# First keys and queries moved in another order, with edits to the softmax sums, the router and the experts' first load

## The reference, cut to what matters

```
# cross-attention, 16 heads of 32, 8192 keys for each batch
q, k, v = heads(layernorm(x) @ Wq), heads(ctx @ Wk), heads(ctx @ Wv)
x = x + (softmax(q k^T / sqrt(32)) v) @ Wo
# causal self-attention: softplus amplitude (normalised per head) and tanh phase
x = x + amp_phase_attention(layernorm(x))
# experts: 16 of them, the best 2 for each token, 64 places for each expert and batch
g = softmax(layernorm(x) @ w_router)           # 16 scores for each token
p1, p2, e1, e2 = top_k(g, 2)                   # place = running count of the expert
x = x + sum over both of p * expert(e, row)    # silu(row @ gate) * (row @ fc) @ proj
```

## Time and profile before

| | us |
|---|---|
| median of 3 runs | 2043.98 |
| the profiled execution, its own time | 2044.43 |
| its span in the profile | 2042.7 |
| PE busy | 1894.5 (93%) |
| DVE busy | 1726.3 (85%) |
| ACT busy | 1469.4 (72%) |
| mean granted clock of PE | 0.971 of full |

### The profile page before, as it was taken

The page is one execution under the profiler, slowest core; times in us unless marked ns, Lnnn a source line. Parts: engine busy times, 40 slices in busy tenths (PEclk is TensorE's granted clock), DMA queues, the critical chain, the costliest instruction groups (busy, mean ns, idle before and its releaser), DMA issues.

```text
span 2042.7 us, 30924 instructions
## 1 busy us (share of the span) xinstructions
PE 1894.5 (93%) x11702; PEld 779.7 (38%) x11702; DVE 1726.3 (85%) x1509; ACT 1469.4 (72%) x1671; POOL 46.3 (2%) x57
## 2 busy tenths in 40 slices
PE   7799999999999999999999999999998989997593
PEld 3333333333333333333333333333332445555482
DVE  5589999999999999788999999999999587786354
ACT  2288888888888888668888888888886546452120
POOL 2000000000000000000000000000000000001103
PEclk9899999999999999999999999999999989999797
DMA  5533332233333323322323333323240000006574
GB/s 192 200 100 92 89 97 84 78 88 90 91 92 86 97 78 105 92 78 58 98 78 83 88 89 93 89 83 99 62 151 15 22 1 2 1 31 228 201 261 145
DMA packets 112584, 194.55 MB, mean 95 GB/s; under 512 B 10288, under 2 KB 63536, under 8 KB 112432
## 3 DMA queue, kind: packets, MB, share of 16 engines
q1 hardware_dynamic: 109872, 184.12, 30.6%
q0 software_dynamic: 2560, 8.39, 1.2%
HBM read 108.58 MB, written 50.33 MB: 78 GB/s over the span
## 4 chain that ended last, share of the span: by engine, by line
PE 80%; DVE 8%; DMA 4%; issue 3%; ACT 2%; SPq 1%; POOL 1%; POOLq 0%; ACTq 0%; DVEq 0%
PE ps L1055 21%; PE ps L1227 21%; PE ps L972 11%; PE ps L969 11%; PE ps L1286 3%; DVE dacc L1657 2%; PE ps L1088 2%; PE ps L1127 2%; PE ps L1083 1%; PE ps L1042 1%; PE ps L1296 1%; DMA kscr<-wsm 1%; PE ps L1152 1%; DMA kst<-kscr 1%; PE ps L1142 1%
## 5 line engine op out<-in xcount | busy, mean ns | idle before, releaser
L1489 ACT ACTIVATE pt<-ps,bias 128x1024 f32<-128x1024 f32 x1024 | 1110.0, 1114 | 222.8 <-PE ps L1227 222.2
L1657 DVE TENSOR_TENSOR dacc<-dacc,pt 128x2048 f32<-128x2048 f32 x504 | 1152.8, 2287 | 50.1 <-ACT pt L1489 25.5
L1227 PE MATMUL ps<-qst,kst 128*128 128x512 f16 x2048 | 614.0, 382 | 20.6 <-ACT pt L1489 19.7
L1055 PE MATMUL ps<-pt,vt 128*32 128x512 f32 x4096 | 494.5, 600 | 1.8 <-ACT pt L1489 1.8
L1227 PEld LDWEIGHTS ps<-qst,kst 128*128 128x128 f16 x2048 | 178.2, 98 | 427.8 <-ACT pt L1489 133.3
L969 PE MATMUL ps<-wsm 128*128 128x512 f16 x1152 | 313.7, 383 | 14.6 <-DVE wsm L1615 10.7
L972 PE MATMUL ps<-wsm 128*128 128x512 f16 x1152 | 312.1, 381 | 5.2 <-ACT vt L1341 2.8
L1055 PEld LDWEIGHTS ps<-pt,vt 128*32 128x32 f32 x4096 | 106.8, 109 | 267.0 <-issue 243.2
L969 PEld LDWEIGHTS ps<-wsm 128*128 128x128 f16 x1152 | 113.0, 99 | 155.8 <-DVE wsm L1615 10.7
L972 PEld LDWEIGHTS ps<-wsm 128*128 128x128 f16 x1152 | 112.9, 98 | 145.2 <-issue 5.3
L1600 DVE SCALAR_TENSOR_TENSOR wsm<-ps,wsm 128x512 f16<-128x512 f32 x128 | 87.7, 686 | 31.8 <-ACT wsm L1337 31.7
(11 more groups left out here) (192 smaller groups left out, 1188.2 us busy)
## 6 DMA issues: line engine op xcount, KB each, us to landing
kscr<-wsm SPq DMA_DIRECT2D x128, 256.0 KB, 3.5
kst<-kscr SPq DMA_DIRECT2D x128, 256.0 KB, 3.5
kst<-kst SPq DMA_DIRECT2D x128, 256.0 KB, 3.4
wsm<-in_ctx SPq DMA_DIRECT2D x32, 768.0 KB, 4.8
qst<-qscr SPq DMA_DIRECT2D x32, 128.0 KB, 2.9
xbuf<-xn SPq DMA_DIRECT2D x16, 256.0 KB, 6.4
wsm<-in_gate SPq DMA_DIRECT2D x8, 512.0 KB, 4.7
wsm<-in_fc SPq DMA_DIRECT2D x8, 512.0 KB, 5.9
```

The source lines that it names most:

```text
L1055: p = e.matmul(ps[32 * h:32 * h + 32, 4 + n % 2, :], vt[:, kb % 2, ch, c:c + 32], pt[:, (2 * i + h // 2) % 6, h % 2, :], start=ch == 0, st ...
L1227: p = e.matmul(ps[:, 2 * half + h2, :], kst[:, kb % 2, h, ch * 128:ch * 128 + 128], qst[:, h, :], start=True, stop=True)
L1489: e.activation(pt[:, (2 * i + half) % 6], ps[:, 2 * half:2 * half + 2, :], ACT.Exp, bias=bias[:, 4 * kb + ch:4 * kb + ch + 1], scale=SCORE ...
L1657: e.tensor_tensor(own_heads, own_heads, probs, ALU.add).then_inc(S["add"], 1)
```

## The change

- Start-up: `k_move` is split for block 0 into `k_store` and `k_load`. The load takes both halves of the partitions from DRAM, without the copy within the core. The order on SP's queue is now: store keys 0, keys 1; load keys 0, keys 1; store queries 0, keys 2; load queries 0, keys 2; store queries 1, keys 3; load queries 1, keys 3; store queries 2, queries 3; load queries 2, queries 3.
- Last key block of batch 1 (16 steps): in the third and fourth chunk of each group DVE no longer adds; PE sums these probabilities with `ones`, four matmuls in a step, straight into the bank of `finish`.
- Last query tile of self-attention (four groups n): DVE adds two of the four key tiles and masks the last one, and PE sums the other two key tiles itself, 8 more matmuls for each n.
- Router: rT now turns the tile x3 as it is, without waiting for statistics; mean and scale are applied to the 16 logits: logit is now two operations, and one product of `wr` with `ones` (colsum) and its negation (negsum) are new, once. In the order of the slots rT, rC, router and logit of tile 6 come later, and at the end rT and rC of tile 7 come ahead of stat and lroot.
- Top 2: 'first' has 3 operations, 'second' 6, 'shares' 4. 'first' needs no exponential, and for the second half of the tokens 'shares' comes after the rows are known. xn3 of the last tile is made behind 'cum'.
- Experts: the four loads of `xe` have 1, 3, 5 and 7 blocks in place of 4 each.

The core of the diff (left out: counts that follow from it, two new small buffers, a constant that is folded into an index):

```diff
@@ -30,6 +30,7 @@
+PARTS = ((0, 1), (1, 4), (4, 9), (9, 16))
@@ -379,6 +380,12 @@
+ON_PE = [i for i in range(STEPS - 16, STEPS) if i % 4 > 1]
+
+
+def added(i):
+
+    return i + 1 - sum(x <= i for x in ON_PE)
@@ -491,6 +498,9 @@
+if not kept:
+    late = {4: ["wo0"], 5: ["wo1"], 6: ["x3", "stat"], 7: ["lroot"], 8: ["lnr", "xn3"], 10: ["rT"], 11: ["rC"],
+            13: ["router"], 14: ["logit"]}
@@ -503,6 +513,11 @@
+if a == 1 and k == 4:
+    out.append(("colsum", 0, fill((1,))))
+    empty((1,), "lg", 1)
+if a == 1 and k == 5:
+    out.append(("negsum", 0))
@@ -510,7 +525,7 @@
-out.append((("rank", "odds", "shares", "first", "second")[(6, 8, 9, 11, 13).index(k)], 0))
+out.append((("rank", "odds", "first", "second", "shares")[(6, 8, 9, 11, 13).index(k)], 0))
@@ -592,13 +607,15 @@
-for step in ("x3", "stat", "lroot", "lnr", "xn3", "rT", "rC", "router", "logit"):
+for step in ("x3", "rT", "stat", "rC", "lroot", "lnr", "router", "logit"):
...
-for what in ("rank", "odds", "shares", "first", "second"):
+for what in ("rank", "odds", "first", "second"):
...
+follow(7, "xn3")
...
+out.append(("shares", 1))
@@ -805,6 +824,16 @@
+def k_store(g):
+    e.wait_ge(S["klo"], g + 1)
+    e.dma_start(kscr[0, g], khl[:, g % 2]).then_inc(S[f"kw{g}"], 16)
+
+def k_load(g):
+    e.wait_ge(S[f"kw{g}"], 16)
+    for half, name in ((0, "kr"), (64, "ku")):
+        e.dma_start(kst[half:half + 64, 0, 4 * g:4 * g + 4, :],
+                    kscr[0, g].rearrange("(h r) t k -> (r t) h k", h=4)).then_inc(S[f"{name}{g}"], 16)
+
@@ -828,17 +857,21 @@
-k_move(0, 0)
-k_move(0, 1)
+k_store(0)
+k_store(1)
+k_load(0)
+k_load(1)
...
+k_store(2)
...
-k_move(0, 2)
+k_load(2)
...
+k_store(3)
...
-k_move(0, 3)
+k_load(3)
...
+q_store(0, 3)
...
-q_store(0, 3)
@@ -884,9 +917,9 @@
-for q in range(4):
-    e.dma_start(xe[:, 4 * q:4 * q + 4, :],
-                xbuf[512 * q:512 * q + 512, :].rearrange("(x p) c -> p x c", p=128)).then_inc(S[f"qx{q}"], 16)
+for q, (lo, hi) in enumerate(PARTS):
+    e.dma_start(xe[:, lo:hi, :],
+                xbuf[128 * lo:128 * hi, :].rearrange("(x p) c -> p x c", p=128)).then_inc(S[f"qx{q}"], 16)
@@ -1027,10 +1060,10 @@
-at = bank(("finish", b, g))
-e.wait_ge(S["add"], 256 * b + 240 + 4 * g + 4)
+at = 6 + BANK_OF["finish", b, g] % 2 if b else bank(("finish", b, g))
+e.wait_ge(S["add"], added(256 * b + 240 + 4 * g + 3))
...
-    p = e.matmul(ps[32 * h:32 * h + 32, at, :], ones[:, 0:32], dacc[:, 4 * g + h, :], start=True,
+    p = e.matmul(ps[32 * h:32 * h + 32, at, :], ones[:, 0:32], dacc[:, 4 * g + h, :], start=b == 0,
@@ -1054,11 +1087,16 @@
+if i in ON_PE:
+    at = bank(("finish", 1, g)) if ch == 2 else 6 + BANK_OF["finish", 1, g] % 2
+    for h in range(4):
+        p = e.matmul(ps[32 * h:32 * h + 32, at, :], ones[:, 0:32], pt[:, (2 * i + h // 2) % 6, h % 2, :],
+                     start=ch == 2, stop=False)
...
-if what in ("turn", "p01", "p23", "p4", "qkT", "wo", "woT", "rT", "router", "score", "scoreT", "cum", "pT"):
+if what in ("turn", "p01", "p23", "p4", "qkT", "wo", "woT", "rT", "router", "colsum", "score", "scoreT", "cum", "pT"):
@@ -1141,9 +1179,14 @@
+alone = range(2, 4) if t == 7 else ()
...
-                 keysum[:, u, h4, :] if qb else pT[:, u, h4, 0:128], start=True, stop=True)
+                 keysum[:, u, h4, :] if qb else pT[:, u, h4, 0:128], start=True, stop=not alone)
+for k in alone:
+    for h4 in range(4):
+        p = e.matmul(ps[32 * h4:32 * h4 + 32, 6, g * 128:g * 128 + 128], ones[:, 0:32],
+                     pT[:, u, h4, k * 128:k * 128 + 128], start=False, stop=k == 3)
@@ -1191,10 +1234,15 @@
-    e.wait_ge(S["xn3"], t + 1)
+    e.wait_ge(S["x3"], t + 1)
...
-        p = e.transpose(ps[:, ev[2], k * 128:k * 128 + 128], xn3[:, t, k * 128:k * 128 + 128], ident[:])
+        p = e.transpose(ps[:, ev[2], k * 128:k * 128 + 128], xs[:, t, k * 128:k * 128 + 128], ident[:])
...
+elif what == "colsum":
+    e.wait_ge(S["late"], 48)
+    for k in range(4):
+        p = e.matmul(ps[:, 1, 0:16], ones[:], wr[:, k, :], start=k == 0, stop=k == 3)
+    p.then_inc(S["rM"], 1)
@@ -1485,7 +1533,7 @@
-e.wait_ge(S["add"], i - 2)
+e.wait_ge(S["add"], added(i - 3))
@@ -1670,6 +1718,8 @@
+if f:
+    e.wait_ge(S["att"], f)
@@ -1791,6 +1841,12 @@
+if n >= 28:
+    e.tensor_tensor(keysum[:, u], block[0], block[1], ALU.add).then_inc(S["dve"], 1)
+    e.wait_ge(S["dve"], own.up())
+    e.tensor_tensor(block[3], block[3], trib[:].unsqueeze(1).to_broadcast([128, 4, 128]),
+                    ALU.mult).then_inc(S["cut"], 1)
+    return
@@ -1827,44 +1883,60 @@
-    e.wait_ge(S["rM"], t + 1)
-    e.tensor_copy(lg[:, t, :], ps[:, ev[2], 0:16]).then_inc(S["lg"], 1)
+    e.wait_ge(S["lstat"], t + 1)
+    e.tensor_scalar(shift[:], negs[:], mv[:, t, 0:1], rs[:, t:t + 1], ALU.mult, ALU.mult).then_inc(S["dve"], 1)
+    e.wait_ge(S["dve"], own.up())
+    e.wait_ge(S["rM"], t + 2)
+    e.scalar_tensor_tensor(out=lg[:, t, :], in0=ps[:, ev[2], 0:16], scalar=rs[:, t:t + 1], in1=shift[:],
+                           op0=ALU.mult, op1=ALU.add).then_inc(S["lg"], 1)
+elif what == "negsum":
+    e.wait_ge(S["rM"], 1)
+    e.tensor_scalar(negs[:], ps[:, 1, 0:16], -1.0, None, ALU.mult).then_inc(S["lg"], 1)
...
-    e.wait_ge(S["lg"], 4 * t + 4)
+    e.wait_ge(S["lg"], 4 * t + 5)
...
+elif what in ("first", "second"):
+    tiles, k = slice(4 * t, 4 * t + 4), 0 if what == "first" else 1
+    back = iot[:, 1, :].unsqueeze(1).to_broadcast([128, 4, 16])
+    e.wait_ge(S["const"], 1)
+    if k == 0:
+        e.wait_ge(S["lgs"], t + 1)
+        e.scalar_tensor_tensor(out=w3[:, tiles], in0=lg[:, tiles], scalar=0.0, in1=back, op0=ALU.is_equal,
+                               op1=ALU.mult).then_inc(S["dve"], 1)
+    else:
+        e.wait_ge(S["pexp"], t + 1)
+        e.scalar_tensor_tensor(out=lg[:, tiles], in0=ohb[:, 0, tiles], scalar=-2.0, in1=pp[:, tiles],
+                               op0=ALU.mult, op1=ALU.add).then_inc(S["dve"], 1)
+        e.wait_ge(S["dve"], own.up())
+        e.tensor_reduce(tp[:, 1, tiles], lg[:, tiles], AX.X, ALU.max).then_inc(S["dve"], 1)
+        e.wait_ge(S["dve"], own.up())
+        e.tensor_tensor(w3[:, tiles], lg[:, tiles], wide(tp[:, 1, tiles]), ALU.is_equal).then_inc(S["dve"], 1)
+        e.wait_ge(S["dve"], own.up())
+        e.tensor_tensor(w3[:, tiles], w3[:, tiles], back, ALU.mult).then_inc(S["dve"], 1)
+    e.wait_ge(S["dve"], own.up())
+    e.tensor_reduce(ei[:, k, tiles], w3[:, tiles], AX.X, ALU.min).then_inc(S["dve"], 1)
+    e.wait_ge(S["dve"], own.up())
+    mark = e.tensor_tensor(ohb[:, k, tiles], wide(ei[:, k, tiles]), back, ALU.is_equal)
+    if k:
+        mark.then_inc(S["ohb"], 1)
+    else:
+        mark.then_inc(S["dve"], 1)
+        e.wait_ge(S["dve"], own.up())
...
+    e.tensor_reduce(tp[:, 0, tiles], pp[:, tiles], AX.X, ALU.max).then_inc(S["dve"], 1)
+    e.wait_ge(S["dve"], own.up())
...
-    e.tensor_tensor(pp[:, tiles], pp[:, tiles], wide(v8[:, tiles]), ALU.mult).then_inc(S["dve"], 1)
+    e.tensor_tensor(tp[:, :, tiles], tp[:, :, tiles], v8[:, tiles].unsqueeze(1).to_broadcast([128, 2, 4]),
+                    ALU.mult).then_inc(S["dve"], 1)
...
-elif what in ("first", "second"):
...
@@ -1917,7 +1989,8 @@
-adds(i)
+if i not in ON_PE:
+    adds(i)
```

More of the change, by code:

```diff
@@ L484, in follow @@
             out.append(("router", f, bank, fill((bank,))))
-            empty((bank,), "lg", f + 1)
+            empty((bank,), "lg", f + 2)
         elif step == "logit":
@@ L673, in build @@
         wr = sb("wr", [128, 4, 16], F32)
+        negs = sb("negs", [128, 16], F32)
+        shift = sb("shift", [128, 16], F32)
         s1 = ExitStack()
@@ L917, in pool @@
             e.iota(iot[:, 0, :], pattern=[[1, 16]], base=0, channel_multiplier=0, allow_small_or_imprecise_dtypes=True)
-            e.iota(iot[:, 1, :], pattern=[[1, 16]], base=100, channel_multiplier=0,
+            e.iota(iot[:, 1, :], pattern=[[1, 16]], base=-100, channel_multiplier=0,
                    allow_small_or_imprecise_dtypes=True)
@@ L1269, in e_turn @@
                 s = x % 2
-                e.wait_ge(S[f"qx{x // 4}"], 128 + 16)
+                e.wait_ge(S[f"qx{next(q for q, (lo, hi) in enumerate(PARTS) if x < hi)}"], 128 + 16)
                 if x > 1:
@@ L1473, in self_piece @@
                     if t:
-                        e.wait_ge(S["rM"], t)
+                        e.wait_ge(S["rM"], t + 1)
                     e.activation(aR[:], ps[:, ev[2], :], ACT.Copy).then_inc(S["rC"], 1)
@@ L1655, in adds @@
                 else:
-                    e.wait_ge(S["add"], i)
+                    e.wait_ge(S["add"], added(i - 1))
                     e.tensor_tensor(own_heads, own_heads, probs, ALU.add).then_inc(S["add"], 1)
@@ L1844, in self_piece @@
                     e.wait_ge(S["dve"], own.up())
-                    e.tensor_tensor(pp[:, tiles], pp[:, tiles], wide(v8[:, tiles]), ALU.mult).then_inc(S["dve"], 1)
+                    e.tensor_tensor(tp[:, :, tiles], tp[:, :, tiles], v8[:, tiles].unsqueeze(1).to_broadcast([128, 2, 4]),
```

(28 more changed lines are left out.)

## The result

| | before | changed |
|---|---|---|
| median, us | 2044.01 (4 runs, 2043.13 to 2045.52) | 2026.64 (4 runs, 2023.89 to 2028.71) |
| ratio to before, 95% interval | | 0.9912 (0.9897 to 0.9927) |
| the profiled execution, own time / span | 2044.43 / 2042.7 | 2023.89 / 2022.1 |
| mean granted clock of PE | 0.971 | 0.978 |

The changed kernel is 17.4 us faster by the medians; 16.4 was forecast (2028.0, range 2023.5 to 2032.5). By the interval of the ratio the gain is 14.9 to 21.1 us. The profiled execution is the fastest of the four, so its differences have to be read against other executions before they are put down to the change.

The account below looks back on a forecast made before the run. PE was taken to bound the kernel in the main loop, so gains come only from the ends: -8.7 - 1.0 + 1.4 - 3.1 - 4.5 - 0.5 = -16.4, from 2044.43 to 2028.0 us, range 2023.5 to 2032.5.

Parts of the forecast that it names:

- Start-up, -8.7: Start-up: the new order on SP's queue leaves PE as the bound, last query split 8.7 us earlier; bounds -6 to -10.
- The remark on the copy: Start-up, second half of the partitions: a load from DRAM landed in 3.4 us, just as the copy within the core did.
- Last key block, -1.0: Last key block: DVE loses 8 adds, the PE and ACT ring sets the pace, 1.0 us saved; bounds -2.5 and +0.9.
- Router within the loop, +1.4: Router in the loop: longer logits, negation and colsum cost 1.4 us; bounds 0 (all covered) and +3.
- my own mark: Sign that the prediction is wrong: the stretch from 1600 to 1860 grows by more than 3 us.
- Last tile, -3.1: Last query tile: fewer DVE adds save 3.0 us less PE's 0.4, exponentials no longer behind rC 0.5; bounds -1.5 and -5.
- x3 to the counts, -4.5: From x3 to the counts: -3.0 us up to the logit, -1.5 behind it; bounds -3.5 and -6.
- Experts' first load, -0.5: Experts' first load: one turn saved, 1.0 us, less 0.5 for later issue of the second piece; bounds -1 and +1.
- the PE sets in series: Rival, last key block: added PE sets do not overlap, +20.4 us, total 2048.4; chance 0.02.
- SP as the bound: Rival, start-up: loads of query groups 2 and 3 land 10 us later, half that gain falls, 2032 us; chance 0.08.
- Nothing from the end: Rival, last tile and router: new DVE operations cost what the chain saves, only start-up and counts remain, 2033 us; chance 0.10.
- PE warm to the end: Rival, behind x3: shorter gaps keep the clock up, transposes and product save 0.5 and 0.9, 2025 us; chance 0.12.

## Why the prediction was right, point by point

- *Start-up, -8.7:* -8.4 to -10.3 in the traces (those with this part), -10.3 by the medians of the kernel with this alone. The mechanism is as forecast (PE is the bound, 4.29 us for each query group, nobody waits for loads). In the first profile the 0.6 more is that the whole chain from 52.95 stands 0.65 earlier. The remark on the copy was right and could have been stronger: even the copy may stay.
- *Last key block, -1.0:* -0.75. Pairs 6.07 us (6.05 came out of the sum), projection 3.70 for 3.5, first projection 0.95 later for 0.7.
- *Router within the loop, +1.4:* this is the term that was mis-sized. From the flag to x3 of tile 6 it was +1.6 to +3.3 instead of +1.4 where the kernel before took 2044 us, and +3.3 to +6.6 on the other two chips, against the one trace of before. By my own mark (more than 3 us in that stretch) this step failed, in the first profile by 0.2. The logits are as put: from behind colsum to x3 of tile 5 it is +1.1 to +1.4 in eleven of the twelve traces with them (+3.0 in one). I had left out two things. In six of ten traces the clock came back later behind colsum, up to 1.7 more. And on the two chips where the kernel before took 2050 us, the stretch of tile 6 has a halt of 1.4 to 1.6 us at a granted clock of 1.00, in seven of eight followed by half clock, up to 4.7 together. My bound of +3 was too low for that. That the change causes the halt is not shown: no trace tells whether the kernel before has it on those chips as well. Cosine waits 5.6 us for DVE now where it waited 3.5; I had reckoned with 1.0 for five logits and 0.2 for the negation:
```profile
L1473 ACT ACTIVATE qc<-t,hpi 128x1024 f32<-128x1024 f32 x7 | 8.0, 1148 | 5.7 <-DVE t L1802 5.6
```
- *Last tile, -3.1:* -2.87 in every trace with the cut. The size is right by luck, the account is not: the cuts brought 1.5 and not 2.6. The other 1.3 comes from elsewhere, by my reading from the wait for xn3 that is gone, where I had put 0.5 for exponentials no longer behind rC; the 3.86 us of that wait I had not seen in the trace.
- *x3 to the counts, -4.5:* -4.3 to -5.3 with this order. My 4.0 us to the logit were counted from the end of x3. Counted so, it was 3.1 where transposes and product ran at full clock, 3.3 to 4.2 elsewhere. Behind the logit it was -1.45 for -1.5. In the first profile the roots no longer hid beside PE's work: the product is done at 1871.33, and the last logit starts at 1871.65, behind DVE's own chain of roots and `shift`.
- *Experts' first load, -0.5:* -1.6 in the first profile, -1.4 to -1.6 at the first product in the traces with these pieces, and -0.4 to -1.7 at the turn of the last block. The turn hides as forecast (1.11 us for 1.97); the term that was mis-sized is the second piece, which landed 0.7 sooner where I had put 0.5 later. The Trainium skill (DMA: Bandwidth & Descriptors, Bandwidth) advises transfers of 1 MiB or more; it measured loads issued from GpSimd, and its aim is a share of peak bandwidth. Here, with loads issued from SP, the trace decides otherwise, as PE waits for the first two blocks: 512, 768 and 1024 KB landed 3.7, 4.7 and 5.7 us behind their issue.
- *The rivals:* the PE sets in series fell (8 records in 1.04 us, pairs 6.07). SP as the bound fell. Nothing from the end fell (last tile and tail together -7.1 to -8.2). PE warm to the end is what the first profile shows, together with a main loop that was shorter, most of it by luck; the median lies between that case and the forecast.

The errors cancelled in part, so that the total came this close is some luck: in the first profile +1.8 in the router against -0.6, -0.8 and -1.1 in start-up, tail and experts. The chip matters as much: 17.4 us of gain in the first comparison and 21.5 on the one where the kernel before took 2050.4 and the changed one 2028.9. Why the gain is larger there stays open, since no trace of the kernel before was taken on it.

## What to carry to other kernels

Where one queue carries stores and loads of several producers, write its order by when each piece is ready and when it is wanted, and batch the waits: stores first, then loads. By the medians that was worth more than all the edits of arithmetic together, and it needed no faster transfer. An algebraic move that takes a dependency away (mean and scale applied behind the product) was worth 2.6 us in the chain behind x3, with the order left as it was (0.45 of it by the clock). Whether it also pays in the middle of the program, where an instruction that waits holds up the queue behind it, stays open here, as a later slot alone would have removed that wait. And an earlier start is worth only what the next bound leaves of it: the first product came up to 1.4 us sooner with smaller pieces, and the last block no sooner.
